# First attention: the row loads of batches 8 to 15 issued from written-out code, and the first maxima sent ahead of the rows of batch 3

## The reference, cut to what matters

```python
x = x + _L0_xattn_ref(_layernorm(x, axis=-1), ctx_1024, ctx_1024, ...)

q = _split_heads(Q @ Wq.T + bq)
k = _split_heads(K @ Wk.T + bk)
v = _split_heads(V @ Wv.T + bv)
scores = jnp.einsum('bhqd,bhkd->bhqk', q, k) / jnp.sqrt(jnp.float32(D_K))
probs = jax.nn.softmax(scores, axis=-1)
out = jnp.einsum('bhqk,bhkd->bhqd', probs, v)
```

## Time and profile before

| | us |
|---|---|
| median of 3 executions | 437.22 (437.04 to 439.81) |
| the profiled execution, device time | 438.72 |
| its span in the profile | 437.0 |
| its mean granted TensorE clock, as a share of full speed | 0.931 |
| before the first attention | 0 to 39 |
| first attention | 39 to 137.5 |
| experts | 137.5 to 279.7 |
| second attention and ternary feed-forward | 279.7 to 437 |

### The profile page before, as it was taken

The page is one execution under the profiler, slowest core; times in us unless marked ns, Lnnn a source line. Parts: engine busy times, 40 slices in busy tenths (PEclk is TensorE's granted clock), DMA queues, the critical chain, the costliest instruction groups (busy, mean ns, idle before and its releaser), DMA issues. The chain is left out here.

```text
span 437.0 us, 10507 instructions
## 1 busy us (share of the span) xinstructions
PE 356.5 (82%) x3434; PEld 256.6 (59%) x3434; DVE 288.8 (66%) x905; ACT 224.7 (51%) x420; POOL 89.9 (21%) x163
## 2 busy tenths in 40 slices
PE   1484677888977999999999999789899999757663
PEld 0352556766763567776677767557677676534442
DVE  5675677988965753574433443696789899367893
ACT  2142345656664664444434343146566656648894
POOL 6335040020203002100101001124333342310000
PEclk9887599999998999999999999889999999856997
DMA  7555864334317000650161100103444331000111
GB/s 200 119 145 126 209 162 129 118 113 119 97 30 240 2 1 5 127 111 1 35 179 41 36 0 0 37 14 108 132 124 113 96 103 29 3 1 1 32 30 37
DMA packets 54100, 34.98 MB, mean 80 GB/s; under 512 B 38744, under 2 KB 46256, under 8 KB 54064
## 3 DMA queue, kind: packets, MB, share of 16 engines
q1 hardware_dynamic: 44032, 31.43, 26.7%
q10 hardware_dynamic: 10032, 3.08, 3.0%
HBM read 24.60 MB, written 9.44 MB: 78 GB/s over the span
## 5 line engine op out<-in xcount | busy, mean ns | idle before, releaser
L1039 ACT ACTIVATE probs<-ps_e 128x512 f32<-128x512 f32 x128 | 75.5, 594 | 60.7 <-PE ps_e L884 55.9
L957 DVE TENSOR_REDUCE neg<-ps_s 128x4 f32<-128x512 f32 x128 | 85.2, 685 | 23.3 <-PE ps_s L867 22.1
L1285 DVE SCALAR_TENSOR_TENSOR x_all<-ps_ym,c_g,x_all 128x128 f32 (+1 forms) x128 | 36.0, 344 | 63.1 <-PE ps_ym L1380 63.0
L1380 PEld LDWEIGHTS ps_ym<-w,hid 128*128 128x128 f32 x512 | 60.8, 192 | 9.2 <-issue 6.7
L1380 PE MATMUL ps_ym<-w,hid 128*128 128x128 f32 x512 | 62.2, 276 | 0.0
L1370 PE MATMUL ps_h<-tok_t,w 128*128 (+1 forms) x128 | 61.9, 607 | 0.0
L1487 ACT ACTIVATE hid<-ps_h,b 128x512 f32<-128x512 f32 x64 | 43.1, 684 | 35.3 <-PE ps_h L1370 33.9
L867 PE MATMUL ps_s<-k_rows,q_rows 96*128 96x128 bf16 x512 | 54.0, 233 | 8.7 <-PEq L448 3.9
L884 PE MATMUL ps_e<-q_rows,k_rows 128*128 128x128 bf16 x512 | 50.6, 224 | 11.0 <-DMA q_rows<-neg_t 10.3
L867 PEld LDWEIGHTS ps_s<-k_rows,q_rows 96*128 96x128 bf16 x512 | 40.1, 104 | 22.2 <-issue 9.6
L884 PEld LDWEIGHTS ps_e<-q_rows,k_rows 128*128 128x128 bf16 x512 | 36.2, 100 | 17.7 <-DMA q_rows<-neg_t 10.1
(11 more groups left out here) (200 smaller groups left out, 552.5 us busy)
## 6 DMA issues: line engine op xcount, KB each, us to landing
k_rows<-k_dram SPq DMA_DIRECT2D x32, 144.0 KB
q_rows<-q_dram SPq DMA_DIRECT2D x32, 144.0 KB
k_rows<-k_dram SPq DMA_DIRECT2D x16, 288.0 KB
q_rows<-q_dram SPq DMA_DIRECT2D x16, 288.0 KB
k_dram<-parts SPq DMA_DIRECT2D x35, 128.0 KB, 2.3
w<-in_w SPq DMA_DIRECT2D x16, 128.0 KB, 2.6
q_dram<-parts SPq DMA_DIRECT2D x15, 128.0 KB, 2.2
q_dram<-parts ACTq DMA_DIRECT2D x9, 128.0 KB, 3.1
```

What stands on the lines that cost most here:

```text
L957: dve.tensor_reduce(neg[:, s, q * HQ:(q + 1) * HQ], ps_s[:, q % 2, :].rearrange("p (h k) -> p h k", h=HQ), AX_X, ALU.max, negate=True).the ...
L1039: act.activation(probs[:, s, q, :], ps_e[:, q % 2, :], ACT.Exp, scale=SCALE).then_inc(exp_done, 1)
L1285: dve.scalar_tensor_tensor(out=batch_of(x_all, g * G + j), in0=ps_y[:, e % 2, j * D:(j + 1) * D], scalar=c_g[:, j, e:e + 1], in1=batch_of( ...
L1380: last = pe.matmul(ps_y[:, e % 2, j * D:(j + 1) * D], hid[:, (e % 2) * M + m, j * P:(j + 1) * P], w2[:, e, m, :], start=(m == 0), stop=(m ...
```

## The change

Two things, both in the order on SP in the first attention.

1. At the block's start `lay_maxima(0)` stands between the rows of batch 2 and those of batch 3. It stood behind both. `lay_maxima(1)` and the store of unit 6 stay behind all of them.
2. The loop over batches 8 to 15 is written out as sixteen half-loads with constant addresses and eight `lay_maxima`. The wait on `last_stored` (units 6 and 7 stored), which stood at the end of each turn of the loop, is now once ahead of batch 12, the first that reads those units. (NG - 1) * G is 12.

```diff
--- before.py
+++ after.py
@@ -807,14 +807,16 @@
 
             if layer == 1:
                 queries.store(sp, last - 1, queries.stored[0])
+            for b in range(2):
+                if layer == 0 and b == 0:
+                    for half in range(2):
+                        load_half(sp, c, AHEAD, AHEAD, half)
+                lay_maxima(b, b)
+                if layer == 0 and b == 0:
+                    for half in range(2):
+                        load_half(sp, c, AHEAD + 1, AHEAD + 1, half)
             if layer == 0:
-                for b in range(AHEAD, SLOTS):
-                    for half in range(2):
-                        load_half(sp, c, b, b, half)
-            for b in range(2):
-                lay_maxima(b, b)
-                if layer == 0 and b == 1:
-                    store_unit(sp, c, LATE[3], c["last_stored"])
+                store_unit(sp, c, LATE[3], c["last_stored"])
 
             if layer == 0:
                 sp.wait_ge(c["parts_stored"], 16 * (K_PARTS + PARTS))
@@ -826,11 +828,10 @@
                     store_unit(sp, c, LATE[4], c["last_stored"])
             if layer == 0:
                 sp.wait_ge(c["late_stored"], 16 * (K_PARTS + PARTS))
-                with sp.Fori(2, B // SLOTS) as i:
-                    for r in range(SLOTS):
-                        load(i * SLOTS + r, r)
-
-                    sp.wait_ge(c["last_stored"], 16 * (K_PARTS + PARTS))
+                for b in range(2 * SLOTS, B):
+                    if b == (NG - 1) * G:
+                        sp.wait_ge(c["last_stored"], 16 * (K_PARTS + PARTS))
+                    load(b, b % SLOTS)
             else:
                 sp.wait_ge(queries.stored[0], 16 * PARTS * 2)
                 for b in range(2 * SLOTS, B):
```

## The result

The changed kernel takes 434.36 us, median of 9 executions (431.3 to 436.14), beside 438.46 us of the kernel before (435.32 to 439.95) on the same chip. The ratio is 0.992, 95% interval 0.989 to 0.9949, so by the ratio about 3.5 us less (2.2 to 4.8). Its profiled execution took 434.39 us with a span of 432.7 us.

What follows compares the result with a forecast made beforehand. The prediction took SP's queue, which lays the maxima PE waits for, as the suspected bound, with DVE full behind it in the loop. Gains of 1.0 + 1.5 = 2.5 us off 437.22 gave 434.7 us, range 432.6 to 437.0.

Steps and rivals of the forecast that it cites:

- The sum, 2.5 us: Gain forecast for the first attention: 1.0 us from the earlier first maxima plus 1.5 us from the written-out loop.
- Both terms: The two forecast gains: 1.0 us at the attention's start, 1.5 us in the stretch of SP's loop.
- ACT stands in the way: Step 0: ACT's store of unit 4 holds the exponentials until 49.52 instead of 50.52, so the gain is 1.0 us.
- takes 47: Start of the attention: the first maxima's DMA was taken to land at 47, between bounds of 46.8 and 48.3.
- My outer bound of 2.2: First part's gain if the last DMA of ACT's store takes 0.88 us: 2.2 us.
- The condition that this would prove me wrong: Step 0: the forecast is wrong if the exponentials do not start when ACT's store ends, expected at 49.5.
- The rival with the quicker store: Start of the attention: ACT's last store DMA takes 0.88 us, giving 1.15 us more, 433.6; chance 0.18.
- the bound of 3.1: First part's gain if ACT did not matter and the end of SP's loads at 48.2 set it: 3.1 us.
- What is late next is DVE: Loop's stretch: with SP's issues cheaper, DVE at some 5.0 us a step sets the pace; PE's waits for it rise.
- the first cycle can shrink to what the second took: Steps 6 to 9 on DVE fall from 21.56 to 20.26 us, a gain of 1.30 us.
- The slower case: From step 0, TensorE's clock stays low; if through step 4, 1.7 us slower, 438.9; chance 0.05.
- the rivals I took in: Within the range: ACT's store quicker (chance 0.18), loop without effect (0.11), first part without effect (0.07).

Runs made afterwards that it cites:

- e3: The kernel before, unchanged, profiled once more for its trace: 438.32 us, one execution.
- e2: Changed kernel with rows of batch 3 again ahead of the first maxima, so only SP's loop written out: 437.7 us, ratio 1.0004 to the kernel before.
- e1: Changed kernel with SP's loop put back, so only the first maxima moved ahead: 434.93 us, ratio 0.9948 to the kernel before.
- e11: Changed kernel with late stores of units 6 and 7 spread behind batches 4 to 10 and ACT's store of unit 4 behind step 1: 434.9 us, ratio 0.9911.
- e8: Changed kernel with ACT's store of unit 4 moved from ahead of step 0 to behind step 1: 434.45 us, ratio 0.9914.
- e5: Kernel before, with DVE's maxima in layer 0 over 64 of 128 keys, leaving out half of the search: 437.16 us, ratio 0.9975.
- e6: Changed kernel, with DVE's maxima in layer 0 over 64 of 128 keys, leaving out half of the search: 429.3 us, ratio 0.9801.
- e9: Changed kernel with the eight late stores of units 6 and 7 behind batches 4 to 10, one each, two behind batch 7: 434.39 us, ratio 0.9923.
- e7: Changed kernel with the eight stores of units 6 and 7 one by one behind batches 6 and 7, two by two behind 8 to 10: 433.55 us, ratio 0.9877.
- e10: The changed kernel itself, timed again on the same chip as versions with spread stores: 433.05 us, ratio 0.9896 to the kernel before.

## Why the prediction was right, and which of its steps were not

The forecast was 434.7 us and the measured medians are 434.36 and 433.05. The sum, 2.5 us, stands beside 2.8 us in the attention of the traces (2.3 to 3.0 with the repeats), and 3.5 and 4.5 us by the timed ratios, whose intervals begin at 2.2 and 2.7. That the number fits so well is luck in two ways. Both terms were off by about a factor of two, in opposite directions. And the forecast was taken off a median of three, 437.22 us, where nine executions beside the changed kernel gave 438.46: off that it would read 436.0.

**First part: 1.0 us forecast, about 2.1 measured.** From the first product to step 6 the old order takes 46.01, 46.00 and 45.48 us (before, e3, e2), mean 45.8; the new one 43.63, 44.27, 44.01 and 43.10, mean 43.75. e1 gives 2.3 us by its timed ratio (1.0 to 3.6). The step that failed is "ACT stands in the way": it rested on one DMA of 2.03 us. Leaving the kernels with the light DVE aside, a store of over 5 us showed in two of the three traces of the old order (5.74, 5.46; 3.80 in e2) and in none of the new order with that store in place (2.87 to 3.73). And where it was long, in e3, it ended before the landing. What set the exponentials was the landing of the first maxima: 4.2, 4.8 and 4.6 us in the old order, 3.1 to 3.6 in the new, and 2.5 and 2.6 with ACT's store out of the way (e11, e8). I had these bounds (2.7 to 4.2, "takes 47") and then let them count for nothing. My outer bound of 2.2, for ACT's DMA at 0.88 us, is what came as a number, but not by that mechanism. What did it is that the first maxima were issued 1.6 us sooner, counted from the first product (4.96 against 6.52 us in the mean), and landed about 1.1 us quicker. That made 2.7 us at the second `lay_maxima`.

**The condition that this would prove me wrong did come**: the exponentials did not start when ACT's store ended but 0.5 us later. The rival with the quicker store (433.6) was nearer in number, but in it too ACT sets the start. Of my terms only the bound of 3.1 had ACT out of the way, and it had the end of SP's loads in its place, where the copy of the maxima came last (ready at 47.60, laid at 47.62).

**The rest of the first part held in the main.** The rows of batch 3 cost nothing. What was won travelled to step 6, but not whole: counted from the first product, the second and the third `lay_maxima` came 2.7 and 2.2 us earlier than before, and step 6 came 2.1 us earlier (means of three traces of the old order and four of the new). The half microsecond between the second and the third is SP's store of unit 6, which took 2.71 and 2.72 us in the two traces of the kernel before and 3.22, 3.44 and 3.46 in the three of the changed one. I had put nothing for that.

**Second part: 1.5 us forecast, 0.7 measured in the old order and 0.2 on top of the first part.** SP's issues of a batch fell from 5.05 to about 4.1 us as worked out, PE's waits for the maxima's DMA went to nothing in the loop (forecast under 0.5 us) and its waits for DVE's maxima rose to 2.7 us (forecast 3 or more), with 2.7 for the split. "What is late next is DVE" is right, and e5 and e6 show it: with DVE lighter, the two cycles of the traces gain 3.5 us. The step that failed is "the first cycle can shrink to what the second took". DVE's own first cycle is longer: 0.35 us at the turn of its loop, which I read as a wait for PE because the profile named PE, and 0.3 us more for one cast beside POOL's work (0.48 at 98.91, 0.17 for the same cast at 103.42 in the profile before). By the traces its floor is 20.9, not 20.26: five of them reach it within 0.02 us, and none goes below with DVE's full work. I had also read the second cycle as free of idle time but for fractions of 0.1 us. It has four gaps of 0.15 to 0.30 us, 0.98 in all, the same in the changed kernel, and the profile lays them to DVE's own results. So they are part of its floor. e2's timed ratio (1.0 us quicker to 1.4 slower) agrees with 0.7 as with 0.2.

**The slower case** was half right. The low level did reach past the 60 us that I had set as proof against me, and a product took 1.94 us. But it did not come by a late rise, as I had it. The clock rose sooner than before, at 50, and fell again when PE waited for the rows of batch 4 (1.68 us) and the maxima of batch 2 (1.40 us). It cost little: 2.2 us were won at the third `lay_maxima`, laid ahead of the fall, and 2.1 at step 6. SP's queue was packed until 61.00, and I take that for the reason. e9 points to the price without that cover: 6.06 - 4.55 = 1.5 us between two maxima, 1.1 without that store.

**Two sums.** Half a microsecond to a side of the rivals I took in gives 433.1 to 436.7, not the 432.6 to 437.0 that I wrote. And the loads of batch 3 start 44.9 - 42.4 = 2.5 us later, not 2.4. Neither changes the forecast.

**What stays open.** The timed ratios give 3.5 to 4.5 us and the attention of the traces 2.3 to 3.0. The stage ahead, in which no edit lies, took 38.53 to 39.11 us in the three traces of the old order and 37.76 to 38.46 in the eight of the new. With the light DVE it is the same way round, 37.85 in e5 and 36.89 in e6. That is 0.7 to 1.0 us which goes with the order on SP in all thirteen traces, and I have no cause for it; no run here tests one. The parts alone, 2.3 us less for e1 and 0.2 more for e2 by the ratios, add up to less than the whole, within intervals of over 1 us. Nor did any run here test why the landing of a 12 KB DMA varies from 2.5 to 4.8 us, beyond that it is long with more queued ahead of it or ACT's store beside it. Nor why the clock fell in the tail of e1 and e7 alone.

## What to carry to other kernels

Before a queue's issue time is cut, ask which engine would be late next, and lighten that engine in a copy of both kernels: e5 and e6 told that the two cycles give 3.5 us when DVE is light, where they give 0.2 to 0.7 behind a full one. A small DMA that a chain hangs on goes ahead of bulk loads in its queue: 2 us for a swap of lines. And the floor of a cycle is not the time of its neighbour until idle times at loop turns and casts beside another engine have been subtracted in both.

## What the runs showed of the hardware

- Issues with addresses worked out from a register start 0.85 to 1.07 us apart, those with constant addresses 0.82. Five of them cost 1 us more a batch.
- A DVE cast of 128 x 16 elements took 2.42 us where it usually takes 0.17, while POOL ran an addition over 128 x 2048 elements at the same time; both ended at 56.9. The kernel before has the same pair (2.37 us at 58.66). In the changed kernel:

```profile
54.53 2.42 DVE L965 CAST neg_parts<-neg 128x16 bf16<-128x16 f32 x1
```

```profile
52.41 4.51 POOL L1115 TENSOR_TENSOR x_all<-x_all,row_bias 128x2048 f32<-128x2048 f32 x1
```

- TensorE's granted clock fell from 1.00 to 0.50 in the midst of the stage in the changed kernel. PE had been busy for 0.4 of the 3 us from 54 to 57, and the clock was down until 63 although PE was full from 58 on. A product of line 899 took 1.94 us there and 1.08 at 50.80.
- The clock can differ between executions in the same work: in the tail of e1 it read 0.50 from 122 to 125 with PE full, and 1.00 in the changed kernel, where PE was full too. It cost some 1.5 us.
- Five issues of one store on ACT's queue took 2.87 us in e10 and 5.74 in the kernel before, one of them alone 2.03. The five issues of SP's store of unit 6 took 2.71 us in the kernel before and 3.46 in e10.
